# Edge tiles of 125 edges in place of 128, in a two-layer graph kernel

## The reference

```
# layer 0: spline convolution
b     = max(1 - |clip(pseudo,0,1) - grid| * 2, 0)        # 2 x 3 factors an edge
basis = outer(b[:,0], b[:,1])                            # 9 an edge
out[dst] += einsum('ek,ei,kio->eo', basis, x[src], weight)   # 9 x 32 x 32
out = out / max(degree, 1) + x @ root_w.T + root_b

# layer 1: tensor-field layer
R   = relu(dist * w1 + b1) @ w2 + b2                     # 64 hidden, 384 radial values an edge
Y   = spherical_harmonics(rel_vec)
msg = products of R, Y and x[src], summed over channels
out[dst] += msg
```

## Time and profile before

| | |
|---|---|
| median of 3 runs | 11184.96 us (11180.47 to 11219.96) |
| span of the profiled execution | 11204.5 us |
| PE busy | 7268.4 us (65%) |
| DVE busy | 5863.1 us (52%) |
| ACT busy | 2726.5 us (24%) |
| POOL busy | 5939.1 us (53%) |
| DMA | 332 MB, 30 GB/s over the span |
| loop of layer 0 | about 40 to 4990 us |
| loop of layer 1 | about 5050 to 11112 us |

### The profile page before, as it was taken

How to read it: one execution, slowest core, us unless ns; L and a number is a source line. 1 busy time by engine, 2 the same in 40 slices (tenths; PEclk the granted TensorE clock), 3 DMA queues, 4 the chain that set the end, 5 groups by cost and what they waited for, 6 DMA issues and landing times. The chain is left out here.

```text
span 11204.5 us, 123807 instructions
## 1 busy us (share of the span) xinstructions
PE 7268.4 (65%) x30515; PEld 3770.5 (34%) x30515; DVE 5863.1 (52%) x14800; ACT 2726.5 (24%) x7061; POOL 5939.1 (53%) x6282
## 2 busy tenths in 40 slices
PE   5555555555555555556777777777777777777777
PEld 2222222222222222233333333333333333333334
DVE  3333333333333333335666666666666666666666
ACT  1000000000000000013333333333333333333333
POOL 5555656555555555554444445444445444444443
PEclk8777777777777777778888888888888888888887
DMA  1111111111111111112111111111111111111111
GB/s 26 13 13 13 13 13 13 13 13 13 13 13 13 13 13 13 13 22 50 43 42 42 43 42 44 42 41 43 41 42 44 43 42 41 43 43 42 43 41 38
DMA packets 640988, 332.17 MB, mean 30 GB/s; under 512 B 522497, under 2 KB 573212, under 8 KB 640718
## 3 DMA queue, kind: packets, MB, share of 16 engines
q0 software_dynamic: 200800, 205.61, 9.7%
q10 hardware_dynamic: 266000, 112.04, 4.9%
q1 hardware_dynamic: 174168, 14.29, 1.2%
HBM read 325.06 MB, written 6.40 MB: 30 GB/s over the span
## 5 line engine op out<-in xcount | busy, mean ns | idle before, releaser
L166 POOL DMA_INDIRECT rows<-table_dram,idx_a x1875 | 1778.6, 949 | 2153.3 <-DVE prods L1010 1563.6
L166 POOL DMA_INDIRECT rows<-in_x,idx_a x1890 | 1786.3, 945 | 1072.9 <-issue 547.3
L897 PE MATMUL sums_ps<-prods,hot 128*64 128x272 f32 x12500 | 1817.9, 442 | 697.3 <-DVE acc L1041 356.8
L581 PE MATMUL sums_all<-spread,hot 128*64 128x289 f32 x6250 | 2039.3, 482 | 112.4 <-DVE spread L459 75.1
L886 PE MATMUL radial_x<-w2p,hidden 128*128 128x384 f32 x3750 | 1703.5, 600 | 506.5 <-DVE prods L1010 462.2
L166 POOL DMA_INDIRECT rows<-table_dram,idx_b x1250 | 1182.4, 946 | 1000.4 <-DVE prods L1010 639.5
L166 POOL DMA_INDIRECT rows<-in_x,idx_b x1260 | 1191.0, 945 | 945.9 <-DVE spread L459 575.0
L897 PEld LDWEIGHTS sums_ps<-prods,hot 128*64 128x64 f32 x12500 | 945.2, 152 | 1589.8 <-issue 792.9
L857 ACT ACTIVATE hot<-window,rel_t 128x64 f32<-128x64 f32 x3125 | 812.8, 335 | 2373.4 <-remote 1753.2
L581 PEld LDWEIGHTS sums_all<-spread,hot 128*64 128x64 f32 x6250 | 943.6, 160 | 909.7 <-issue 472.7
L886 PEld LDWEIGHTS radial_x<-w2p,hidden 128*128 128x128 f32 x3750 | 805.3, 230 | 1072.8 <-issue 413.9
(11 more groups left out here) (148 smaller groups left out, 5749.7 us busy)
## 6 DMA issues: line engine op xcount, KB each, us to landing
dist_ab<-in_edge_weight ACTq DMA_DIRECT2D x125, 480.0 KB
dist_ab<-in_edge_weight ACTq DMA_DIRECT2D x125, 320.0 KB
rows<-in_x,idx_a POOLq DMA_INDIRECT x1890
rows<-table_dram,idx_a POOLq DMA_INDIRECT x1875
rows<-in_x,idx_b POOLq DMA_INDIRECT x1260
rows<-table_dram,idx_b POOLq DMA_INDIRECT x1250
vec_s<-in_edge_attr ACTq DMA_DIRECT2D x125, 37.5 KB
idx_a<-in_src SPq DMA_DIRECT2D x251, 7.5 KB
```

The costliest lines, as they stand in the source:

```text
L166: pool.indirect_dma_start(out=rows[u][:, j, 0:width], out_offset=None, in_=table, in_offset=bass.IndirectOffsetOnAxis(ap=idx[u // 3][:, u ...
L581: last = pe.matmul(sums_ps[s][0:WINDOW, 0:K + 1], hot[s][:, j, :], spread[s][:, j, :], start=(j == 0), stop=(j == G - 1))
L897: last = pe.matmul(sums_ps[s][k * WINDOW:(k + 1) * WINDOW, 0:HALF], hot[s][:, j, :], prods[s][:, j, MUL + 16 * k:MUL + 16 * (k + 1), :].re ...
```

## The change

A new constant EP = 125 takes the place of P = 128 wherever a partition is an edge. T becomes 400000 / 125 = 3200 tiles and B 128 batches; G, U, the slots and every instruction stream stay. Every buffer of edges, every gather, index load and stream load has 125 partitions, a unit has 625 edges, and `hidden` and `dist_ab` have 625 columns for a unit. Buffers with one batch on each partition have PL = 128 partitions now, so `dst_i` comes with one DMA. The loads of nodes and the stores keep their two parts (112 and 13).

```
-T = E // P
+EP = 125
+T = E // EP
-            "idx": [sbuf("idx_a", [P, 3, G], I32), sbuf("idx_b", [P, 2, G], I32)],
+            "idx": [sbuf("idx_a", [EP, 3, G], I32), sbuf("idx_b", [EP, 2, G], I32)],
-EDGES = G * P
+EDGES = G * EP
-        rows = ring("rows", [P, G, C], n=U)
-        spread = ring("spread", [P, G, K + 1])
-        hot = ring("hot", [P, G, WINDOW])
+        rows = ring("rows", [EP, G, C], n=U)
+        spread = ring("spread", [EP, G, K + 1])
+        hot = ring("hot", [EP, G, WINDOW])
-        dst_s = sbuf("dst_s", [P, U, G], I32)
-        pos_s = sbuf("pos_s", [P, U, G * 2])
-        vec_s = sbuf("vec_s", [P, U, G * 3])
+        dst_s = sbuf("dst_s", [EP, U, G], I32)
+        pos_s = sbuf("pos_s", [EP, U, G * 2])
+        vec_s = sbuf("vec_s", [EP, U, G * 3])
...
-            for lo, hi in ROWSPLIT:
-                sp.dma_start(dst_i[lo:hi, :], by_batch[lo:hi, :]).then_inc(dst_landed, 16)
+            sp.dma_start(dst_i[:, :], by_batch[:, :]).then_inc(dst_landed, 16)
...
-            sp.dma_start(base_f[:, :], spans_dram.rearrange("(o b) w -> o (b w)", o=1).to_broadcast([P, B * TW])).then_inc(base_landed, 16)
+            sp.dma_start(base_f[:, :], spans_dram.rearrange("(o b) w -> o (b w)", o=1).to_broadcast([EP, B * TW])).then_inc(base_landed, 16)
...
-        rows = [sbuf(f"rows1_{n}", [P, G, ROW]) for n in range(U)]
-        dist_ab = sbuf("dist_ab", [P, 3 * G * P])
+        rows = [sbuf(f"rows1_{n}", [EP, G, ROW]) for n in range(U)]
+        dist_ab = sbuf("dist_ab", [P, 3 * EDGES])
-        hidden = ring("hidden", [P, G * P])
-        hot = ring("hot1", [P, G, WINDOW])
+        hidden = ring("hidden", [P, EDGES])
+        hot = ring("hot1", [EP, G, WINDOW])
...
-                        last = pe.matmul(radial[h][:, j, 0:R], hidden[s][:, (j0 + j) * P:(j0 + j + 1) * P], w2p[:, :],
+                        last = pe.matmul(radial[h][:, j, 0:R], hidden[s][:, (j0 + j) * EP:(j0 + j + 1) * EP], w2p[:, :],
```

More of the change, by code:

```diff
@@ L85, in build_program @@
             "acc": sbuf("acc", [P, 12800]),
[L87 to L88 removed]
+            "rel_t": sbuf("rel_t", [EP, T]),
+            "rho_t": sbuf("rho_t", [EP, T, 3]),
             "nodes": sbuf("nodes", [P, NJ * C]),
             "ident": sbuf("ident", [P, P]),
[L92 to L93 removed]
+            "iota": sbuf("iota", [EP, WINDOW]),
+            "window": sbuf("window", [EP, WINDOW]),
             "level": sbuf("level", [48, C]),
             "share": sbuf("share", [48, 1]),
[L96 removed]
+            "base_f": sbuf("base_f", [EP, B * TW]),
             "base_now": sbuf("base_now", [1, B * TW]),
@@ L709, in _ @@
                     q0, q = PARTS[n - 2]
-                    here = table[:, q0 * ROW:(q0 + q) * ROW].rearrange("p (q k w) -> p q k w", k=6, w=16)
+                    here = table[0:NP, q0 * ROW:(q0 + q) * ROW].rearrange("p (q k w) -> p q k w", k=6, w=16)
                     part = part_of(nodes, n - 2)
@@ L742, in sem @@
             return ctx.enter_context(nc.semaphore(name))
-        rows = [sbuf(f"rows1_{n}", [P, G, ROW]) for n in range(U)]
-        dist_ab = sbuf("dist_ab", [P, 3 * G * P])
+        rows = [sbuf(f"rows1_{n}", [EP, G, ROW]) for n in range(U)]
+        dist_ab = sbuf("dist_ab", [P, 3 * EDGES])
         DIST = ((0, 3), (3, U))
-        dist = [dist_ab[HID * h:HID * (h + 1), (u - DIST[h][0]) * G * P:(u - DIST[h][0] + 1) * G * P] for u, h in enumerate((0, 0, 0, 1, 1))]
-        hidden = ring("hidden", [P, G * P])
-        hot = ring("hot1", [P, G, WINDOW])
-        rho5 = ring("rho5", [P, G, 5])
-        one = sbuf("one", [P, 1])
+        dist = [dist_ab[HID * h:HID * (h + 1), (u - DIST[h][0]) * EDGES:(u - DIST[h][0] + 1) * EDGES] for u, h in enumerate((0, 0, 0, 1, 1))]
+        hidden = ring("hidden", [P, EDGES])
+        hot = ring("hot1", [EP, G, WINDOW])
+        rho5 = ring("rho5", [EP, G, 5])
+        one = sbuf("one", [EP, 1])
         red = ring("red", [P, 2 * 16])
-        along = sbuf("along", [P, G, MUL])
-        prods = ring("prods", [P, G, OUTS, I17])
+        along = sbuf("along", [EP, G, MUL])
+        prods = ring("prods", [EP, G, OUTS, I17])
         w2p = sbuf("w2p", [P, R])
         w2raw = sbuf("w2raw", [HID + 1, R])
-        dots, turn_a, turn_b = [sbuf(name, [P, G, 3, MUL]) for name in ("dots", "turn_a", "turn_b")]
+        dots, turn_a, turn_b = [sbuf(name, [EP, G, 3, MUL]) for name in ("dots", "turn_a", "turn_b")]
         w1c, b1c = sbuf("w1c", [P, 1]), sbuf("b1c", [P, 1])
-        radial = [psum("radial_x", [P, X, 512]), psum("radial_y", [P, Y, 512])]
+        radial = [psum("radial_x", [EP, X, 512]), psum("radial_y", [EP, Y, 512])]
         sums_ps = [psum(f"sums1_ps{n}", [P, 512]) for n in range(SLOTS)]
@@ L781, in load_dist @@
             u0, u1 = DIST[h]
-            part = edge_weight[bass.ds(i * (U * G * P) + u0 * G * P, (u1 - u0) * G * P)]
-            eng.dma_start(dist_ab[HID * h:HID * (h + 1), 0:(u1 - u0) * G * P],
-                          part.rearrange("(o e) -> o e", o=1).to_broadcast([HID, (u1 - u0) * G * P])
+            part = edge_weight[bass.ds(i * (U * EDGES) + u0 * EDGES, (u1 - u0) * EDGES)]
+            eng.dma_start(dist_ab[HID * h:HID * (h + 1), 0:(u1 - u0) * EDGES],
+                          part.rearrange("(o e) -> o e", o=1).to_broadcast([HID, (u1 - u0) * EDGES])
                           ).then_inc(dist_landed[h], 16)
@@ L851, in body @@
                         act.wait_ge(radial_ready[1], freed(g, u))
-                        act.activation(hidden[s][0:HID, :].rearrange("h (j p) -> h j p", p=P), dist[u].rearrange("h (p j) -> h j p", j=G), ACT.Relu, bias=b1c[HID * h:HID * (h + 1), 0:1],
+                        act.activation(hidden[s][0:HID, :].rearrange("h (j p) -> h j p", p=EP), dist[u].rearrange("h (p j) -> h j p", j=G), ACT.Relu, bias=b1c[HID * h:HID * (h + 1), 0:1],
                                        scale=w1c[HID * h:HID * (h + 1), 0:1]
```

45 lines of the change are left out of this document (20 added, 25 removed).

## The result

| | before | after |
|---|---|---|
| time, median of 4 runs each on one chip | 11,188.97 us (11,180.47 to 11,219.96) | 9,886.44 us (9,885.25 to 9,889.64) |
| profiled execution: span | 11,204.5 us | 9,884.1 us |
| first layer, a batch | 39.6 us x 125 | 37.9 us x 128 |
| second layer, a batch | 48.5 us x 125 | 38.2 us x 128 |
| a gather on POOL, median | 945 ns | 1209 ns |

What follows compares the result with a forecast made beforehand. The prediction saw a cycle: POOL's gathers, a tail until data land and PE's results are seen, then DVE. Terms 264 + 204 + 112 = +580 us on 11,185 gave 11,765 us, range 11,560 to 11,960 (chance 0.45).

Steps and rivals of the forecast that it cites:

- I let an instruction cost what it did: Both loops: instructions keep their cost with 125 partitions, so the loops grow by 128/125, +264 us.
- mean on POOL still 945 ns: Gathers on POOL: mean duration stays 945 ns; a move of more than 20 ns would show the prediction wrong.
- POOL's own time is inside the cycle: Both loops: POOL's gathers, 31.2 us a batch, are followed by a tail and a stretch of DVE.
- The unexplained row: First layer: DVE has 18.28 us without work, waiting for PE; left unexplained, said to be used only in the bounds.
- The last of the signs of being wrong: Both layers: prediction is wrong if waits for PE's results change length with the new grouping of DMA traffic.
- Three batches more, +264: Both loops: three batches more in each, at 39.6 and 48.5 us a batch, +264 us.
- The stream loads, +204: First layer: loads go to five engines, not sixteen, landing 1.9 us later where DVE waits, +204 us.
- The gathers' data later, +112: End of gather runs: five engines land data 0.18 and 0.53 us later; middle of 0 and +224 us taken.
- A: Loads and gathers: only the batch count costs, small descriptors hidden or serial, landing as before; 11,449 us, chance 0.20.
- B: Gathers on POOL: dearer for a count no multiple of 16; 12,853 us, or 12,130 at a third; chance 0.17.
- C: Gathers on POOL: cheaper with five engines, 0.16 to 0.17 us less each, so faster, 10,677 us; chance 0.14.
- D: Both loops: a second pass would double everything, but the number of passes stays one; no chance given.

Runs made afterwards that it cites:

- e4: Kernel after, but each gather fetches 128 rows into buffers of 128 partitions, three of them unused: 11,245.76 us, ratio 1.0195 to the kernel before.
- e3: Kernel before with only its index and stream loads cut to 125 partitions, gathers still of 128 rows: 11,014.95 us, ratio 0.9989.
- e2: Kernel before with only its gathers cut to 125 rows, the rows left out being zero: 9,628.18 us, ratio 0.8729.
- e17: Kernel after, unchanged, run again on one chip beside the best paced kernel: 9,849.20 us, ratio 0.8925 to the kernel before.
- e9: Kernel before with five POOL memsets of 128x2 behind each gather of 128 rows: 9,732.54 us, ratio 0.8825.
- e16: Kernel before with five POOL memsets of 128x2 behind each gather in the first layer, six in the second: 9,548.53 us, ratio 0.8653.
- e15: Kernel before with twelve POOL memsets of 128x2 in one piece behind the fifth gather of each unit: 10,371.72 us, ratio 0.9244.
- e8: Kernel before with three POOL memsets of 128x4 behind each gather of 128 rows: 10,753.70 us, ratio 0.9621.
- e12: Kernel before with gathers of 124 rows, which go to 4 engines, the rows left out keeping zeros: 10,109.96 us, ratio 0.9167.
- e5: Kernel before with two POOL memsets of 128x4 behind each gather of 128 rows: 11,119.81 us, ratio 0.9948.

## Why the prediction was wrong, point by point

**The step that failed** is the one on the gathers: "I let an instruction cost what it did", "mean on POOL still 945 ns". It measured 1209. The prediction named this as a sign that it would be wrong, and by its own sensitivity ("each 10 ns is 64 us") 264 ns on 6400 gathers would have been +1690 us. The time went the other way by 1300 us. So the second error is the greater: the sentence "POOL's own time is inside the cycle". I took the waits for late results as a fixed tail to which POOL's time adds. They weren't fixed. They came with the dense gathers, and a slower POOL took them away.

**The unexplained row.** "DVE waits 18 us for a PE that shows little work" stood in the earlier trace rows as remote, and 4.49 us of the second layer's tail in the earlier trace rows too. I wrote that these rows don't explain it and that I "lean on it only in the bounds", but no bound uses it, and it stayed in the 39.6 and 48.5 us of the sum. The last of the signs of being wrong, that these waits "change their length", is what came true. Over the execution, waits of this kind were 8618 us on two engines. A wait of that size whose cause isn't known belongs in the sum as a term with two ends, 0 among them. With it, the low end would have been POOL's own pace, 128 x 31.2 x 2 + 192 = 8,180 us, and 9,886 would have been in the range.

**Three batches more, +264.** Right in kind; e4 against e3 has +231, and with the other gathers the kernel after has 6 batches of 37.9 us more than e2, 227 us (spans: 9848.3 in e17 against 9617.8).

**The stream loads, +204.** The packets and the five engines were as forecast, the landing 1.2 us later for 1.9, and the cost nothing (e3: -0.3% to +0.1%), in a kernel where DVE does wait for this load. In the kernel after it doesn't, once in 128 batches, since it waits for gathers. What covers the later landing in e3, I can't show. DVE's wait for the load is no longer than before, 341 us, so it reaches that wait later by as much; the remote waits ahead of it, 5058 us in the first layer, leave room for that.

**The gathers' data later, +112.** Five engines with data and sixteen completions, as half forecast (32 packets a gather in the first layer). The last completion comes 1.16 us behind the gather's end on POOL for 1.10 in the first layer, 1.50 for 1.21 in the second (medians): +0.06 and +0.29 where +0.18 and +0.53 were forecast. It costs nothing, since the spacing of the gathers sets the pace.

**The rivals.** A (count only) is what the change would be without its gathers, e4. B (dearer gather on POOL) had its premise right, 264 ns more, and its sign wrong. C (faster than before) had the sign, by the opposite mechanism, a cheaper gather; its premise is refuted. D: one pass, as said. None of the rivals was what happened: a dearer gather that makes the kernel faster. In the chances, the 0.04 for no change is called a part of C; they add up to one only if it stands beside C's 0.14.

**What is shown and what isn't.** Shown: the gathers alone do it (e2); without them the gain is gone (e4); slowing POOL without touching gathers or tiles does the same (e9, e16); and over all kernels the late results of the first layer are nearly gone from an own pace of 36.8 us a batch on, and there at 36.1 and below. Below the edge their amount doesn't follow the pace alone (e15). Not shown is why PE's results are seen late at all when POOL runs ahead of the loop, nor, for the whole time, that the lateness is the cause and not a companion of POOL's stops: no run takes it away and leaves POOL's pace. In the stretch shown it stands on the path, since DVE goes on 0.2 us after PE's increment is recorded, and POOL when DVE has built the next `spread`. In the second layer, where 1170 of the 1300 us were gained, the pace orders the table less well (gathers to 11 and 7 engines, with 32.8 and 35.1 us, take 44.4 and 42.2 us a batch; memsets with 34.6 and 34.8 take 46.3 and 48.7). The kernel after had late results in the second layer on one chip and none on another, with 9,886 and 9,849 us. What these waits are in the hardware stays open, and so does the part of PE's clock in it: it is 0.84 in the second loop before and 0.97 to 0.98 in e2, e16 and after, and by the two stretches PE is busy there for 36 us a batch before and 32 after, 4 of the 10 us gained. The rows above show the clock falling after the wait has begun, not ahead of it, and in the first layer it can't be what makes results late: it is 0.72 to 0.76 in all kernels, with late results (before 0.73, e8 0.75) or without (e12 0.74, e9 0.76). For the second layer no run separates the two.

## What to carry to other kernels

When a wait's end is given to nothing that ends on the core, and PE is idle while its consumers wait, don't add the producer's time to it: try first whether the wait depends on how densely another engine issues. A POOL that waits for DVE 3300 us in all has slack, and a few dummy memsets behind each of its DMAs are a cheap test (e9: 12% faster), if the distance is measured and not reckoned: two of them (e5) moved it by 0.01 us and the time by 0.5%. A change can win by slowing an instruction that looks critical, and then the same slowing without the change is the better kernel: undo everything but the delay and time that.

## What the runs showed of the hardware that I had not expected

- An indirect gather's time on POOL grows as fewer DMA engines get its rows: 945 ns (16), 986 (15), 1009 (11), 1102 (7), 1209 (5), 1290 (4). It doesn't depend on the bytes of a row (128 or 384), and hardly on the rows (112 rows on 16 engines: 933).
- A gather of 125 rows of 128 bytes has 5 packets of 3200 bytes, 11 of 100 bytes and 16 completions of 4. With 384-byte rows it has 10 of 4224 and 5 of 1152, 22 of 44, 11 of 12 and the 16. The data packets add up to 125 rows; the small ones are there beside them on the eleven engines left.
- Loads by the hardware queue with 125 partitions go to five engines as well (1875 packets and 15 completions for three of them), and land 1.2 us later in 4.1 us.
- Memsets of 128x2 behind each other on POOL take 113 to 117 ns each, but twelve of them together 0.44 us: each begins 29 ns behind the one before (39 ns for 128x4).
- The semaphores by which ACT and DVE wait for PE rose late in the kernel before and in PE's order: a copy on ACT began up to 25 us after the end of its matmuls, 8.4 us on average.
